# Position-wise mixture of experts: half-width units, one copy for a pair of PSUM banks

## What is computed

```
h   = layernorm(x)                                   # [32 batch, 64 positions, 256]
g   = gates of each position                         # [64, 8], from mean over the batch
W1s = sum over e of g[s, e] * eW1[e]                 # per position, 1024 x 256
b1s = sum over e of g[s, e] * eb1[e]
W2s = sum over e of g[s, e] * eW2[e]                 # per position, 256 x 1024
b2s = sum over e of g[s, e] * eb2[e]
x   = x + relu(h[:, s] @ W1s.T + b1s) @ W2s.T + b2s
```

## Time and profile before

| | us |
|---|---|
| median of 3 runs | 2796.37 |
| lowest and highest run | 2793.72, 2798.17 |
| span of the profiled execution | 2792.1 |
| this stage, first transpose to last update of X (start of L2032 to end of L2254) | 452.9 to 829.9 |
| two half blocks, from A1 to A1 and from A0 to A0 | 22.19, 22.46 |

### The profile page before, as it was taken

The page is one execution under the profiler, slowest core; times in us unless marked ns, Lnnn a source line. Parts: engine busy times, 40 slices in busy tenths (PEclk is TensorE's granted clock), DMA queues, the critical chain, the costliest instruction groups (busy, mean ns, idle before and its releaser), DMA issues. The chain is left out here.

```text
span 2792.1 us, 84762 instructions
## 1 busy us (share of the span) xinstructions
PE 2517.8 (90%) x36489; PEld 2135.0 (76%) x36489; DVE 1702.0 (61%) x3422; ACT 1391.3 (50%) x3486; POOL 733.8 (26%) x1078
## 2 busy tenths in 40 slices
PE   7999888999968999999998859978997878999988
PEld 6888656777756899999987659977776656999577
DVE  6877675666656333333335755657885777777663
ACT  4888324455532444444432324427884454777342
POOL 3222102212102300000001213423446535666300
PEclk9999999999989999999999969988999999999999
DMA  3110003212031100000000043334320003111000
GB/s 97 36 36 21 1 4 94 63 33 63 3 87 47 36 17 17 17 17 17 2 2 25 4 150 101 127 108 141 93 66 1 2 2 99 48 53 49 1 1 31
DMA packets 118228, 126.76 MB, mean 45 GB/s; under 512 B 10877, under 2 KB 110152, under 8 KB 117864
## 3 DMA queue, kind: packets, MB, share of 16 engines
q1 hardware_dynamic: 114024, 110.93, 13.0%
q0 software_dynamic: 3840, 10.49, 1.2%
HBM read 105.67 MB, written 15.73 MB: 43 GB/s over the span
## 5 line engine op out<-in xcount | busy, mean ns | idle before, releaser
L1157 ACT ACTIVATE s_ca_probs<-s_ca_scores,s_ca_neg_max 128x256 f32<-128x256 f32 x768 | 353.4, 478 | 35.0 <-DVE s_ca_neg_max L1203 25.7
L1203 DVE TENSOR_REDUCE s_ca_neg_max<-s_ca_scores 128x4 f32<-128x1024 f32 x192 | 233.8, 1219 | 46.1 <-PE s_ca_scores L1056 24.7
L2212 DVE COPY s_mx_w_mixed<-s_mx_ps 128x512 f32<-128x512 f32 x256 | 163.7, 684 | 93.5 <-PE s_mx_ps L2058 80.0
L1073 PE MATMUL s_ca_probs_flipped<-identity,s_ca_probs 128*128 128x128 f32 x1536 | 210.6, 280 | 1.7 <-ACT s_ca_probs L1157 1.7
L1073 PEld LDWEIGHTS s_ca_probs_flipped<-identity,s_ca_probs 128*128 128x128 f32 x1536 | 164.4, 141 | 40.2 <-issue 20.8
L2167 ACT COPY s_mx_w_mixed<-s_mx_ps 128x512 f32<-128x512 f32 x256 | 137.4, 589 | 106.6 <-PE s_mx_ps L2045 86.0
L1157 ACT ACTIVATION_READ_ACCUMULATOR s_ca_probs<-s_ca_scores,s_ca_neg_max 128x1 f32 x768 | 160.5, 209 | 0.0
L1164 ACT COPY s_ca_probsT<-s_ca_probs_flipped 128x512 f32<-128x512 f32 x192 | 115.4, 601 | 77.4 <-PE s_ca_probs_flipped L1073 77.3
L971 POOL TENSOR_TENSOR s_ca_inv_spread<-s_ca_inv_sums,h_ca_own_half 128x128 f32<-128x128 f32 x192 | 72.6, 399 | 287.2 <-DVE s_ca_inv_sums L1225 287.2
L82 PE MATMUL s_cc_shared<-s_cc_ctxT_low,h_cc_wkv_high 128*128 128x256 f32 x512 | 146.0, 285 | 2.2 <-DVE s_cc_ctxT_low L1556 2.2
L300 POOL TENSOR_SCALAR x_normed_transposed<-x_normed_transposed,h_cc_rstd,h_cc_shift 128x256 f32<-128x256 f32 x56 | 30.6, 556 | 446.1 <-PE s_cc_out L1450 271.1
(11 more groups left out here) (571 smaller groups left out, 7561.2 us busy)
## 6 DMA issues: line engine op xcount, KB each, us to landing
h_ca_ctxT<-in_ctxT SPq DMA_DIRECT2D x96, 256.0 KB, 3.4
h_mx_w_by_input<-in_L_ffn_eW1T SPq DMA_DIRECT2D x16, 512.0 KB, 5.6
h_mx_w_by_hidden<-in_L_ffn_eW2T SPq DMA_DIRECT2D x8, 1024.0 KB
h_re_win<-in_L_ffn_W_in SPq DMA_DIRECT2D x8, 1024.0 KB, 6.0
h_ca_ctx<-in_ctx SPq DMA_DIRECT2D x32, 256.0 KB, 2.8
x_normed_transposed<-in_ctx SPq DMA_DIRECT2D x7, 1024.0 KB, 5.3
h_re_wout<-in_L_ffn_W_out SPq DMA_DIRECT2D x8, 512.0 KB, 3.8
choice_results<-s_rt_zeros SPq DMA_DIRECT2D x4, 1024.0 KB, 10.6
```

Source lines behind the costliest of these rows:

```text
L1073: last = nc.tensor.transpose(psT[u % len(psT)][:, 2 * a + c, :], PR[b % 2][:, 4 * n + 2 * h + a, c * P:(c + 1) * P], ident[:, :])
L1157: last = nc.scalar.activation(PR[b % 2][:, p, :], psS[:, p // 2, (p % 2) * NKEY:(p % 2 + 1) * NKEY], ACT.Exp, bias=nmax[b % 2][:, p:p + 1] ...
L1203: nc.vector.tensor_reduce(nmax[b % 2][:, 4 * n:4 * n + 4], psS[:, 2 * n:2 * n + 2, :].rearrange("p r (g k) -> p r g k", g=GR), AX_X, ALU.m ...
L2212: last = nc.vector.tensor_copy(part(int(name[1]), r), bank(j, r))
```

## The change

The same eight blocks are now worked through in four units each, 32 units (`u`): two for the first weights, each with half of the block's 128 hidden columns, and two for the second weights, each with half of the 256 output columns; every unit has all 64 positions. What differs:

- **Mixing** (`mix`): four jobs for a unit, each eight matmuls with 32 rows of weights and 256 moving columns, still in the four row groups at once. The mixing of unit `u + 1` is spread between the quarters of unit `u`.
- **Banks**: six banks are three pairs for the mixing, two banks serve the small jobs one by one. Row groups 0 and 1 write one pair, 2 and 3 the next. `reorder1` and `reorder2` permute the columns in groups of 32, so that a pair of banks is one access pattern, and ScalarE copies each first pair with one 128x1024 instruction, VectorE each second. A mix waits for ScalarE's copy of the mix before it and for VectorE's copy of the one before that.
- **Small jobs**: `A`, `F` (the flip), `Y`, `T1` and `T2` come in quarters of one bank. A quarter of `A` has 32 matmuls with 64 columns, of `Y` 16 with 128 columns, and four bias matmuls go ahead of it, all four in row group `n`, since the four share a bank. T1 and the flip are ScalarE's, T2 and Y VectorE's; a block has one buffer for the turned second weights where there were two.
- **GpSimd**: the reordering is 8 and 8 instructions of 128x256 for a block instead of two of 128x1024 and one of 128x2048.
- **End**: Y is stored by halves of its columns, the first half (all positions) one unit before the end; the second half in two pieces. VectorE adds the first half of the columns and ten tiles of the second, GpSimd the last six tiles of the second.

The diff, cut to its core:

```diff
@@ reorder1
-            last = pool.tensor_copy(self.W1R[:, c, :, :], self.W1N[:, c, :, :].rearrange("p e o -> p o e"))
+            for a in range(4):
+                cols = slice(32 * a, 32 * a + 32)
+                last = pool.tensor_copy(self.W1R[:, c, cols, :].rearrange("p (q r o) e -> p q r o e", q=2, r=4),
+                                        self.W1N[:, c, :, cols].rearrange("p e (r q o) -> p q r o e", q=2, r=4))
...
@@ position_experts
-        S = [ps("mx_ps", [P, 4, 512]) for _ in range(2)]
+        PAIR = [ps("mx_mix_ps", [P, 2, 512]) for _ in range(3)]
+        SM = [ps("mx_small_ps", [P, 512]) for _ in range(2)]
...
+                def mix(u, n):
+                    ob, half, m = u // 4, u % 2, 4 * u + n
+                    if n == 0 and u % 4 == 0:
+                        pe.wait_ge(s_small_act, emptied(BY_ACT, PLACE[("T1", ob, 3)]))
+                    if n == 0 and u % 4 == 2:
+                        pe.wait_ge(s_small_dve, emptied(BY_DVE, PLACE[("T2", ob, 3)]))
+                    if m >= 1:
+                        pe.wait_ge(s_mix_act, m)
+                    if m >= 2:
+                        pe.wait_ge(s_mix_dve, m - 1)
+                    for q in range(2):
+                        for r in range(4):
...
+                            last = nc.tensor.matmul(PAIR[(2 * m + r // 2) % 3][:, r % 2, q * 256:(q + 1) * 256], w,
+                                                    GB[rows, :, :, :].rearrange("p k s o -> p (k s o)"), start=True, stop=True)
...
+                def apply1(u, n):
...
-                        nc.tensor.matmul(dst[:, j, 0:P], gates(k, 4 * a + j, j), EB1[32 * j:32 * j + E, ob * P:(ob + 1) * P],
-                                         start=True, stop=False)
+                        nc.tensor.matmul(dst[:, i * OH:(i + 1) * OH], gates(4 * n + i, n), EB1[32 * n:32 * n + E, at:at + OH], start=(i == 0), stop=False)
...
-                    for r in range(2):
-                        last = nc.scalar.copy(part(int(name[1]), r), bank(j, r))
-                    last.then_inc(s_act, 1)
+                    nc.scalar.copy(part(u, n, 0), banks(u, n, 0)).then_inc(s_mix_act, 1)
...
-                    for r in range(2, 4):
-                        last = nc.vector.tensor_copy(part(int(name[1]), r), bank(j, r))
-                    last.then_inc(s_dve, 1)
+                    nc.vector.tensor_copy(part(u, n, 1), banks(u, n, 1)).then_inc(s_mix_dve, 1)
```

More of the change, by code:

```diff
@@ L370, in reorder2 @@
         pool.wait_ge(self.s_w2, 16 * (ob + 1))
[L371 removed]
+        for n in range(8):
+            cols = slice(32 * n, 32 * n + 32)
+            last = pool.tensor_copy(self.W2R[:, cols, :].rearrange("p (q r d) e -> p q r d e", q=2, r=4),
+                                    self.W2N[:, :, cols].rearrange("p e (r q d) -> p q r d e", q=2, r=4))
+        last.then_inc(self.s_r2, 1)
     def prepare(self, pool):
@@ L1944, in position_experts @@
[L1944 to L1960, removed]
+    OH, DH = P // 2, DIM // 2
@@ new lines, in quarters @@
+    def quarters(u):
+        jobs = []
+        if u % 4 == 2:
+            jobs.append(("F", u - 1, 3))
+        for n in range(NQ):
+            jobs.append(("A" if u % 4 < 2 else "Y", u, n))
+            if u % 4 == 0:
+                jobs.append(("T2", u // 4, n))
+            if u % 4 == 1 and n >= 1:
+                jobs.append(("F", u, n - 1))
+            if u % 4 == 2 and u // 4 + 1 < OB:
+                jobs.append(("T1", u // 4 + 1, n))
+        return jobs
+    SMALL = [("T1", 0, n) for n in range(NQ)] + [j for u in range(NU) for j in quarters(u)]
@@ new lines, in mixed2, with order @@
+        def mixed2(u):
+            return MIXED[u % 2][:, :].rearrange("p (s d) -> p s d", s=SEQ)
+        def order(u):
+            mixes = [("M", u + 1, n) for n in range(NQ)] if u + 1 < NU else []
+            smalls = quarters(u)
+            out = mixes[0:1]
+            n = 0
+            for j in smalls:
+                if j[0] in ("A", "Y") and n:
+                    out += mixes[n:n + 1]
+                out.append(j)
+                n += j[0] in ("A", "Y")
+            return out
@@ new lines, in part, with banks @@
+            def part(u, n, pair):
+                if u % 4 < 2:
+                    c, a = n // 2, n % 2
+                    return mixed1(u)[:, c, :, :].rearrange("p s (a k i o) -> p a k i s o", a=2, k=2, i=4)[:, a, pair]
+                return mixed2(u)[:, :, :].rearrange("p s (n k i o) -> p n k i s o", n=4, k=2, i=4)[:, n, pair]
+            def banks(u, n, pair):
+                return PAIR[(2 * (4 * u + n) + pair) % 3][:, :, :].rearrange("p r (q s o) -> p (r q) s o", q=2, o=4)
+            @block.scalar
```

409 lines of the change are left out of this document (168 added, 241 removed).

## The result

The changed kernel takes 2865.3 us (median of 4 runs, 2858.5 to 2869.1), the kernel before 2796.7 us beside it (4 runs, 2793.7 to 2798.2): a ratio of 1.0238, 95% interval 1.0222 to 1.0253, 68.6 us more. The forecast was 2851, +54.5; the result lies inside its range of 2836 to 2866, at the upper edge. The profiled execution took 2863.6 us with a span of 2861.8, which is 69.7 more than the earlier trace rows. In every run that lists both, the time is 1.7 to 2.0 us above the span, so only about 1.8 of the 4.3 us between median and span of before lie around the span; the rest is scatter between executions. From the page: its head, and three groups (line, engine, operation, shapes, count | busy us, mean ns of one | idle before it).

The account below looks back on a forecast made before the run. TensorE's stream was taken as the bound. Eight blocks +45.6, start +4.1, first block's bias for Y +5.3, last block -0.5 give +54.5; with the 2792.1 us span and 4.3 to the median, 2851 us, range 2836 to 2866.

Parts of the forecast that it names:

- What bounds: In the changed stage, TensorE's stream sets the pace; copies matter only where it waits for them.
- The bias: Bias jobs in one row group: 0.94 us each instead of 0.43, twice as many, +5.8 us a block.
- The likeliest case: Whole kernel at 2851 us, with a range of 2836 to 2866; chance 0.70.
- the load-bound rows: Eight weight loads with 8 columns streamed took 0.81 us, about 0.10 each; basis of the 0.94 us bias price.
- the upper bound from the earlier trace: Bias job: load and stream don't overlap in one row group, 1.32 us a job, 2878 in all; chance 0.10.
- the lower of 0.43: Bias job: eight loads in one row group cost no more than before, 0.43 us, 2814 in all; chance 0.09.
- Mixes, applies, transposes: TensorE's other jobs: mixes 0.95 or 1.08 us, apply quarters 1.03, transpose quarters 0.60.
- the faster case: Gaps between TensorE's jobs come from late releases and vanish, as do bias loads; 2762 us in all; chance 0.06.
- Waits: TensorE waiting for copies, per block: four of 0.28 us in the fourth unit, one of 0.87, one of 0.96; 2.9 us.
- The start: Start of the stage: turn, wait and four mixes each waiting for the last one's copy, 12.3 us against 8.2, +4.1.
- The end: End of the stage: Y's turn lands about 3 us later, a shorter update offsets it; 0, bounds -2 and +3.
- the clearing of semaphores: Outside the stage: one more clearing of semaphores with its barrier, put at nothing because no row prices it.

Follow-up runs that it names:

- e5: The changed kernel with each pair copy split into two instructions; ratio 1.0256 to the kernel before.
- e6: The kernel before with reordered columns and one copy for a pair of banks behind each mix, all else kept; ratio 1.0001.
- e7: The kernel before with reordered columns and one copy for a pair of banks behind mixes and turns; ratio 0.9995.
- e1: The kernel before with the four bias matmuls of a job all reading one row group; 2821.0 us against 2799.1.
- e2: The changed kernel with a quarter's bias as one 32-row matmul against a block diagonal; 2838.5 us, ratio 1.0134 to the kernel before.
- e10: The changed kernel without its bias matmuls; 2808.9 us, ratio 1.0030 to the kernel before.
- e9: The kernel before with six semaphores added to the count that triggers clearings, no stage edited; ratio 1.0025, 7.0 us over the kernel before.
- e4: The changed kernel with its six additional semaphores left out of the count that triggers clearings; ratio 1.0193 to the kernel before.
- e11: The kernel before with turns and second applies signalling filled banks to the copying and adding engines earlier; 2781.3 us, ratio 0.9929.
- e3: The changed kernel with each quarter of a turn ahead of its apply instead of behind; 2855.8 us, ratio 1.0199 to the kernel before.

## Why the prediction was right, and where it was not

- **What bounds.** Right: TensorE's stream, both times. e5, e6 and e7 show that the copies as such are worth 1.6 to 3 us of the part.
- **The bias**, the costly term: 0.94 forecast, 0.93 measured. e1 shows the cause, e2 the remedy. e10 bounds the size: all bias jobs together are 54.7 us of the part, and the kernel before had some 16 us of its own, so the change added between 39 (54.7 - 16) and 51 (64 x 0.93 + 8 x 0.98 - 16) of the 53.5 us. The likeliest case took its price from the load-bound rows, and that was the right neighbour; the upper bound from the earlier trace rows and the lower of 0.43 are both out. The Trainium skill, "TensorE: Matmul & The Clock Gate", Part 3, "What overlaps and what doesn't", allows a load under running matmuls only in another row group; these runs disagree for one row group, above all e1, where eight records of 256 columns take 1.81 us, 0.23 each, while the loads alone would add 0.10 to each. No run has the four in different row groups of one bank, so whether sharing a bank forces them into one row group, as the change takes it, is not shown.
- **Mixes, applies, transposes**: 0.95 and 1.08 forecast, 0.98 and 1.07 measured; 1.03 and 1.03; 0.60 and 0.59 (by its own terms the 0.60 is 1.90 - 12 x 0.107 = 0.62). The passages between jobs stayed, so the faster case is out.
- **Waits**: 0.28 forecast for the fourth unit, 0.17 measured; 0.87 and 0.96 forecast, 0.68 and 0.78 measured, each too long by 0.1 to 0.2: from a copy's end to TensorE the prediction took 0.14, and here it is 0.05. The block was forecast too long by 0.3 where one apply takes 1.34 (630.12 - 628.78 in the block above) and by 0.6 in the later blocks, 3 to 4 us over eight.
- **The start** was mis-sized. The chain of copies was right, but the prediction kept the clock at 1.00 in the whole stage, and named a lower one among the things that would make it wrong; behind the waits of the chain it fell for 10.2 us. In each of the seven profiled executions with this start it falls there, for 6.8 to 10.2 us, and in none of the seven with the old start, so the chain is the likely cause, though no run fills its gaps. From the first turn to the first bias it is 15.1 us against 10.5 before, +4.6, and bias, apply and turn behind it lose another 2.1: 6.7 where +4.1 was forecast. That the sum for the part still came out within 1 us is luck: the block's excess and this loss stand against each other.
- **The end**: the step that put it at nothing failed. From the last result to the last fetch's landing it is 17.4 us (868.89 to 886.25) against 11.9 (813.43 to 825.29), 5.5 more where about 3 was forecast; SP's late second store is 2.6 of them. The update behind it takes 3.15 us, not 1.5 to 2, since its last piece went to GpSimd (3.10), so it wins back 1.5 and not 3.
- **Outside the stage**: the clearing of semaphores was named and left without a price. By the places where the time goes it is less the one more barrier than the others moved: 10.3 us in this trace, 7.0 and 12.6 by the runs of e9 and e4, about 7 where scatter is set aside. Of the 15.2 us by which the span's growth exceeds the forecast, 10.3 lie here, 4.0 at the end and 1.9 ahead of the stage, less 1.0 in the part. The range of 2836 to 2866 was reasoned from waits, gaps and the ends alone, so that the result still falls into it is luck too.

## What to carry to other kernels

When a tile is made narrower, look for the small matmuls that come along with it: a job of eight weight loads costs its loads if they share a row group, however few columns it streams, and the count of jobs doubles. A cheaper instruction on an engine that waits for another is worth its saving only at the waits that end at it; an earlier signal to the late engine was worth 18 us of the part against 1.6 (e11, e6). And a stage's semaphores can move what happens in other stages: compare the traces beyond the changed part before explaining a total.

## What the runs showed of the hardware that was not expected

- Records in one row group cost, in these rows, the longer of load and stream: eight take 0.93, 1.05 and 1.81 us with 64, 128 and 256 columns, two take 0.52 with 256 and 0.95 with 512. In four row groups eight records with 128 columns shared the time (0.43).
- TensorE's clock fell to 0.50 in the middle of a full program, in a stage whose start left it idle for 3.5 of 9.2 us, and was back at 1.00 10.2 us later (6.8 in e2, e3 and e10).
- Where the barriers of all engines stand decided about 7 us of a program of 2800 (the stretch behind 1890: 901.3 to 906.1 against 911.1 to 914.3 us), with one barrier more.
